# A state-space and feed-forward layer on one core: new order tables for all engines, a third buffer of halves, later weights as five transfers

## The reference, cut to what matters

```python
x = L0_attn_u                                   # (8, 1024, 256), float32
x = x + mixer(layernorm(x))
x = x + ffn(layernorm(x))

def mixer(u):                                   # 8 heads of 64, state 16
    zxbcdt = u @ W_in.T                         # z0, x0, xBC (544), dt (8)
    dt = softplus(dt + dt_bias);  A = -exp(A_log)
    xBC = silu(causal_conv4(xBC) + conv_b)      # x, B, C
    h_t = exp(dt_t A) h_(t-1) + dt_t x_t B_t    # a scan over 1024 positions
    y_t = C_t h_t + D x_t
    y = layernorm(y) * ln_gamma + ln_beta
    y = sigmoid(y @ W_gate.T + b_gate) * y
    return concat(silu(z0) * x0, y) @ W_out.T

def ffn(x):                                     # weights ternary: -1, 0, 1
    h = layernorm(gelu(x @ absmean(W_fc))) * ln_w + ln_b
    return h @ absmean(W_proj)
```

## Time and profile before

| | |
|---|---|
| median of three runs | 1202.77 us (1202.25 to 1202.82) |
| the profiled execution | 1201.22 us; its span 1199.4 us |
| mean granted clock of TensorE | 0.977 |
| PE busy | 1128.5 us (94% of the span), 8534 matmuls |
| DVE busy | 995.9 us (83%) |
| ACT busy | 957.9 us (80%), of it 138.6 us in 108 table loads |
| POOL busy | 406.5 us (34%) |
| chain that ended last | PE 69%, DVE 13%, ACT 6%, DMA 4% |

### The profile page before, as it was taken

The page is one execution under the profiler, slowest core; times in us unless marked ns, Lnnn a source line. Parts: engine busy times, 40 slices in busy tenths (PEclk is TensorE's granted clock), DMA queues, the critical chain, the costliest instruction groups (busy, mean ns, idle before and its releaser), DMA issues.

```text
span 1199.4 us, 23100 instructions
## 1 busy us (share of the span) xinstructions
PE 1128.5 (94%) x8534; PEld 724.5 (60%) x8534; DVE 995.9 (83%) x1958; ACT 957.9 (80%) x1665; POOL 406.5 (34%) x500
## 2 busy tenths in 40 slices
PE   4678999999999999999999999999999999999996
PEld 1345566657576665757666575766657476666663
DVE  5899997989889898988979798988979888676664
ACT  5666587987879888797878988798887878687855
POOL 1111315153343424243341524333243322524341
PEclk9787999999999999999999999999999999999998
DMA  5610202242333424253342434234154320332444
GB/s 150 199 44 11 72 18 64 50 103 45 88 72 58 94 52 98 45 96 67 64 89 51 101 55 94 58 54 107 27 109 78 79 55 8 91 71 65 95 89 106
DMA packets 238976, 89.14 MB, mean 74 GB/s; under 512 B 207760, under 2 KB 235152, under 8 KB 238864
## 3 DMA queue, kind: packets, MB, share of 16 engines
q1 hardware_dynamic: 238864, 87.67, 33.8%
HBM read 24.32 MB, written 8.39 MB: 27 GB/s over the span
## 4 chain that ended last, share of the span: by engine, by line
PE 69%; DVE 13%; ACT 6%; DMA 4%; issue 3%; SPq 3%; POOL 0%; DVEq 0%; ACTq 0%; POOLq 0%
PE bank L360 39%; PE bank L587 8%; PE bank L575 7%; PE bank L509 4%; DVE cv L949 3%; PE bank L518 2%; PE bank L425 2%; PE bank L494 2%; PE bank L526 1%; DMA hT<-hb 1%; DVE EM L1064 1%; SPq L1280 1%; DVE hb L1134 1%; DMA x3T<-hb 1%; PE bank L469 1%
## 5 line engine op out<-in xcount | busy, mean ns | idle before, releaser
L360 PE MATMUL bank<-xnT,win 128*128 128x512 f16 (+1 forms) x1248 | 305.4, 392 | 18.9 <-DMA xnT<-hb 18.2
L360 PEld LDWEIGHTS bank<-xnT,win 128*128 128x128 f16 (+1 forms) x1248 | 124.2, 103 | 153.2 <-issue 34.4
L949 DVE SCALAR_TENSOR_TENSOR cv<-bank,cws,cv 128x510 f32<-128x510 f32 (+5 forms) x240 | 178.8, 745 | 11.2 <-ACT cv L672 2.6
L360 PE MATMUL bank<-yhl,wg 128*128 128x512 f16 x768 | 173.4, 379 | 2.1 <-DVE yhl L1087 2.1
L180 ACT ACT_TABLE_LOAD x108 | 138.6, 1283 | 1.9
L587 PE MATMUL bank<-wpj,hT 128*128 128x256 f16 x1024 | 126.4, 278 | 12.9 <-DMA hT<-hb 12.9
L575 PE MATMUL bank<-wfc,x3T 128*128 128x512 f16 x512 | 127.0, 381 | 4.0 <-DMA x3T<-hb 4.0
L360 PEld LDWEIGHTS bank<-yhl,wg 128*128 128x128 f16 x768 | 73.9, 98 | 92.5 <-issue 4.5
L1206 POOL TENSOR_TENSOR cat<-sz,cat 128x512 f16<-128x512 f32 x64 | 82.6, 1291 | 128.1 <-ACT cat L786 128.1
L1202 POOL TENSOR_TENSOR caty<-tg,caty 128x512 f16<-128x512 f32 x64 | 83.6, 1306 | 118.6 <-ACT caty L774 118.6
L587 PEld LDWEIGHTS bank<-wpj,hT 128*128 128x128 f16 x1024 | 99.7, 99 | 35.3 <-issue 15.6
(11 more groups left out here) (146 smaller groups left out, 2138.2 us busy)
## 6 DMA issues: line engine op xcount, KB each, us to landing
x<-in_x SPq DMA_DIRECT2D x32, 512.0 KB, 4.1
out_y<-x SPq DMA_DIRECT2D x15, 512.0 KB, 3.0
crep<-cv SPq DMA_DIRECT2D x128, 32.0 KB, 2.0
hT<-hb SPq DMA_TRANSPOSE x128, 3.1
caty<-in_wg SPq DMA_DIRECT2D x1, 1024.0 KB, 7.0
x<-in_wout SPq DMA_DIRECT2D x1, 1024.0 KB, 9.4
hT<-in_wfc SPq DMA_DIRECT2D x1, 1024.0 KB, 12.2
hn<-in_wpj SPq DMA_DIRECT2D x1, 1024.0 KB, 13.2
```

Source lines behind the costliest of these rows:

```text
L360: m = eng.matmul(b, lhs(p, k), rhs(q, k), start=(n == 0), stop=(n == len(seq) - 1))
L949: op = eng.scalar_tensor_tensor(cs[0:w, j, 3 - k:T], b[0:w, 0:T - 3 + k], cws[0:w, j, k:k + 1], cs[0:w, j, 3 - k:T], ALU.mult, ALU.add)
```

## The change

All five order tables are new; each holds the same steps with the same parts as before (SP's has five more words, since `W` and `K` now come in parts). Steps of one activation table stand side by side in ScalarE's. `halves` has a third buffer: x keeps `halves[0]`, x2 gets `halves[2]`, and `before_halves0` is gone. `weights` issues one of its five transfers each time that a `W0` comes, `constants` three of its six at each `K0`. Some steps get a further wait. Of the tables the first lines stand here:

```diff
 PE_ORDER = (
-    "c00 z01 u02 c03 c04 v05 c06 c07 z01 v00 m02 c13 x05 z04 x06 x01 u17 e00 s02 c15 b04 q036 x07 c11 g00 c12 "
-    "q053 t06 O07 v04 c11 r002 w0 q067 w0 q053 r046 w0 w0 m17 y05 z03 z10 c22 v04 x16 y07 x11 u20 c26 e14 y05 x12 "
...
+    "c00 c01 u02 v03 c04 z05 c06 c07 z00 m02 z01 c14 v05 c10 x06 x07 x03 v02 u16 x01 e07 s05 c12 c16 c13 q074 g05 "
+    "b07 q004 t01 O05 z00 z17 r042 q016 w0 w0 q035 m11 r063 c25 w0 w0 g11 x14 y02 y00 y07 x16 y03 u24 v02 s16 x11 "
...
 ACT_ORDER = (
-    "a0 h0 W0 N0 W0 c0 z0 c0 b0 c0 a1 h1 c0 10 c0 30 l0 z0 40 s0 s0 50 l0 c1 z0 e0 f0 D0 c1 E0 c1 F0 c1 F0 11 a2 "
-    "h2 E0 31 c1 E0 E0 l0 b1 O0 s1 41 s1 z0 O0 c2 51 y0 z1 c2 y0 e1 f1 E1 y0 c2 y0 E1 n0 c2 l0 n0 12 a3 h3 n0 n0 "
...
+    "N0 a0 h0 W0 W0 c0 c0 c0 a1 10 h1 30 c0 c0 z0 z0 s0 40 b0 s0 l0 c1 50 z0 e0 c1 c1 D0 f0 E0 11 c1 E0 c1 F0 F0 "
+    "a2 O0 h2 31 E0 E0 41 l0 l0 s1 b1 s1 51 z0 z1 c2 y0 y0 f1 y0 E1 E1 e1 y0 12 a3 32 n0 n0 n0 n0 l0 E1 c2 c2 E1 "
...
 DVE_ORDER = (
-    "a0 h0 W0 N0 Z0 W0 a1 c0 u0 c0 v0 00 c0 h1 c0 20 40 c0 v0 50 a2 60 x0 c1 x0 u1 x0 e0 D0 c1 x0 b0 c1 01 g0 c1 "
...
+    "a0 h0 N0 W0 Z0 W0 a1 c0 u0 00 c0 c0 20 h1 40 c0 c0 v0 a2 50 x0 x0 60 v0 v0 u1 x0 c1 01 c1 x0 g0 b0 E0 E0 c1 "
...
 POOL_ORDER = (
-    "a0 a1 l0 H1 a2 l0 c1 c1 c1 c1 l0 c1 y0 y0 y0 y0 a3 l0 k0 k0 k0 k0 y1 H3 a4 c3 y1 c3 y1 y1 c3 c3 l1 c3 k1 l1 "
...
+    "a0 a1 l0 H1 c1 c1 a2 l0 c1 c1 l0 c1 y0 y0 y0 y0 a3 k0 H3 k0 l0 k0 k0 y1 y1 y1 y1 c3 c3 l1 c3 c3 a4 c3 V0 l1 "
...
 SP_ORDER = (
-    "h0 h0 K0 c0 h1 h1 W0 60 h2 h2 c1 61 h3 c2 h3 r0 62 r1 X0 X0 c3 h4 h4 j0 63 j0 j0 j0 j0 j0 j0 j0 c4 X1 X1 p0 "
-    "r2 64 h5 h5 j1 j1 j1 j1 j1 j1 j1 j1 c5 X2 p1 X2 r3 h6 h6 65 j2 j2 j2 j2 j2 j2 j2 j2 X3 X3 c6 p2 h7 h7 r4 j3 "
...
+    "h0 h0 W0 K0 K0 h1 h1 W0 c0 60 W0 W0 h2 h2 c1 61 h3 h3 62 r0 c2 X0 X0 W0 h4 r1 h4 63 c3 j0 j0 j0 j0 j0 j0 j0 "
+    "j0 p0 X1 h5 X1 h5 r2 64 j1 c4 j1 j1 j1 j1 j1 X2 j1 j1 X2 p1 r3 h6 h6 65 j2 c5 j2 j2 j2 j2 j2 j2 X3 X3 c6 j2 "
...
-        halves = [sb(f"hb{n}", [P, 2, 1024], f16) for n in range(2)]
+        halves = [sb(f"hb{n}", [P, 2, 1024], f16) for n in range(3)]
...
-        HALVES0 = [("hx".index(letter), i) for letter, i, _, _ in steps_of(ACT_ORDER) if letter in "hx"]
...
             def bias_rows(i, n, at):
...
+                pe.wait_ge(gam_v, 3)
...
             def half_x(i, n):
...
-                before_halves0(i, 0)
+                act.wait_ge(xt_hi, 16 * i)
+                act.wait_ge(xn_lo, i)
...
             def half_x2(i, n):
...
-                before_halves0(i, 1)
-                eng.activation(halves[0][:, 0, :], x2[:, i % 2].rearrange("p c d -> p (c d)"), ACT.Copy
+                act.wait_ge(x3t_hi, 16 * i)
+                act.wait_ge(x2_lo, i)
+                eng.activation(halves[2][:, 0, :], x2[:, i % 2].rearrange("p c d -> p (c d)"), ACT.Copy
...
-            def before_halves0(i, which):
-                for kind, k in HALVES0[:HALVES0.index((which, i))][-1:]:
-                    act.wait_ge((xt_hi, x3t_hi)[kind], 16 * (k + 1))
-                    act.wait_ge((xn_lo, x2_lo)[kind], k + 1)
...
             def gelu_h(i, n):
...
+                if half == 0:
+                    act.wait_ge(h_sq, at - 1)
...
             def ternary(i, n):
...
+                dve.wait_ge(gam_v, n + 1)
...
             def bias_halves(i, n):
...
+                dve.wait_ge(gam_v, 2)
...
             def var_x(i, n):
...
+                dve.wait_ge(x_var, i)
...
             def rest_x(i, n):
...
-                before_halves0(i, 0)
+                dve.wait_ge(xt_lo, 16 * i)
...
             def rest_x2(i, n):
...
-                before_halves0(i, 1)
-                eng.tensor_tensor(halves[0][:, 1, :], x2[:, i % 2].rearrange("p c d -> p (c d)"), halves[0][:, 0, :],
+                dve.wait_ge(x3t_lo, 16 * i)
+                eng.tensor_tensor(halves[2][:, 1, :], x2[:, i % 2].rearrange("p c d -> p (c d)"), halves[2][:, 0, :],
...
-            def before_halves0(i, which):
-                for kind, k in HALVES0[:HALVES0.index((which, i))][-1:]:
-                    dve.wait_ge((xt_lo, x3t_lo)[kind], 16 * (k + 1))
...
             def dt_last(i, n):
...
+                dve.wait_ge(xd, 4 * (i - 1))
...
             def c_grown(i, n):
...
+                dve.wait_ge(s_done, i)
...
             def b_suffix(i, n):
...
+                dve.wait_ge(seg_l, i + 1)
+                dve.wait_ge(s_done, i)
...
             def gram_mask(i, n):
...
+                dve.wait_ge(em, 4 * i)
...
             def advance(i, n):
...
+                dve.wait_ge(ce, i + 1)
...
             def y_rows(i, j):
...
+                dve.wait_ge(y_lo, 4 * i)
...
             def var_y(i, c):
...
+                dve.wait_ge(y_var, at - 3)
...
+                dve.wait_ge(yn, at - 3)
...
             def var_x2(i, n):
...
+                dve.wait_ge(x2_var, i)
...
             def load_x(i):
...
-            def constants(i, n):
-                for q in range(2):
-                    eng.dma_start(ahl[:, q, :, :, :], c16_d[:, 0:256].rearrange("p (q c r) -> p q c r", q=2, c=NCH)
-                                  ).then_inc(ld_c16, 16)
-                    eng.dma_start(segR[:, q, :, :], c16_d[:, 256:1280].rearrange("p (e t) -> p e t", e=8)
-                                  ).then_inc(ld_c16, 16)
-                    eng.dma_start(pick[:, 2 * q:2 * q + 2, :, :],
-                                  c16_d[:, 1280 + 256 * q:1536 + 256 * q].rearrange("p (c e m) -> p c e m", c=2, e=8)
-                                  ).then_inc(ld_c16, 16)
+            def constants(i, q):
+                eng.dma_start(ahl[:, q, :, :, :], c16_d[:, 0:256].rearrange("p (q c r) -> p q c r", q=2, c=NCH)
+                              ).then_inc(ld_c16, 16)
+                eng.dma_start(segR[:, q, :, :], c16_d[:, 256:1280].rearrange("p (e t) -> p e t", e=8)
+                              ).then_inc(ld_c16, 16)
+                eng.dma_start(pick[:, 2 * q:2 * q + 2, :, :],
+                              c16_d[:, 1280 + 256 * q:1536 + 256 * q].rearrange("p (c e m) -> p c e m", c=2, e=8)
+                              ).then_inc(ld_c16, 16)
...
             def weights(i, n):
...
-                eng.dma_start(wgs, wg_d.rearrange("(k p) n -> p k n", p=P)).then_inc(ld_wg, 16)
-                eng.dma_start(wos, wout_d.rearrange("(k p) n -> p k n", p=P)).then_inc(ld_wout, 16)
-                eng.dma_start(wfs.rearrange("p (k n) -> p k n", k=2), wfc_d.rearrange("(k p) n -> p k n", p=P)
-                              ).then_inc(ld_wfc, 16)
-                eng.dma_start(wps.rearrange("p (k n) -> p k n", k=8), wpj_d.rearrange("(k p) n -> p k n", p=P)
-                              ).then_inc(ld_wpj, 16)
-                eng.dma_start(lnwb[:, :], lnw_d).then_inc(ld_lnw, 16)
+                if n == 0:
+                    eng.dma_start(wgs, wg_d.rearrange("(k p) n -> p k n", p=P)).then_inc(ld_wg, 16)
+                elif n == 1:
+                    eng.dma_start(wos, wout_d.rearrange("(k p) n -> p k n", p=P)).then_inc(ld_wout, 16)
+                elif n == 2:
+                    eng.dma_start(wfs.rearrange("p (k n) -> p k n", k=2), wfc_d.rearrange("(k p) n -> p k n", p=P)
+                                  ).then_inc(ld_wfc, 16)
+                elif n == 3:
+                    eng.dma_start(wps.rearrange("p (k n) -> p k n", k=8), wpj_d.rearrange("(k p) n -> p k n", p=P)
+                                  ).then_inc(ld_wpj, 16)
+                else:
+                    eng.dma_start(lnwb[:, :], lnw_d).then_inc(ld_lnw, 16)
...
             def turn_x(i, n):
...
+                    sp.wait_ge(z_mm, 4 * (i - 2))
...
             def turn_x2(i, n):
...
-                eng.dma_start(x3T[:, n, :, :, :].rearrange("p c k t -> p (c k) t"), halves[0][:, n, :], transpose=True
+                eng.dma_start(x3T[:, n, :, :, :].rearrange("p c k t -> p (c k) t"), halves[2][:, n, :], transpose=True
...
```

## The result

The changed kernel takes 1182.49 us (median of 4 runs, 1182.05 to 1182.58) where the kernel before takes 1202.51 us: 0.9834 of it, 95% interval 0.9818 to 0.9850. A second group of runs gave 0.9832 (0.9815 to 0.9848). The profiled execution took 1182.05 us, its span is 1180.3 us.

A forecast was written before the change was run, and what follows sets the result against it. The prediction took TensorE to bound the middle and VectorE the stretch from 60 to 150 us. From 1201.2 us it took 4 (start), 4 (middle) and 0 (end), giving 1193.2; plus 1.55 for the median, 1195 us (1189 to 1200).

The forecast's parts named there:

- segR, 4.3 us: Start: with later weights in five transfers, TensorE's wait for segR's rows ends at 47.8 instead of 52.1 us, 4.3 us gained.
- the forecast's other reckoning: Start: by ring order wout still delays segR's rows, so splitting the weights gives 2.6 us and not 4.3.
- `ahl`, 2.2 us: Start: the new table order on ScalarE and VectorE removes 2.2 us of TensorE's 4.6 us wait for `ahl`.
- I take 4 us as gained at the start: Start: of 4.3 + 2.2 us, 4 us come through because VectorE is nearly full from 60 to 150 us; ends 0 and 11.
- VectorE's table now puts 3 us less work ahead of `y2`.: Start: moving `D0` and other steps leaves VectorE 176.4 instead of 179.4 us of work before its `y2` step.
- The half clock: Up to 180 us: some 36 us run at 1.2 GHz; if early holes close, TensorE holds 2.4 GHz for longer.
- Table loads, 0 us: ScalarE: switches fall from 108 to 95, 16.7 us less, hidden behind TensorE's fixed 948 us and so costed at 0.
- rival D: Whole kernel: the compiler keeps more than 95 table loads; within 2 us of the forecast, no chance of its own.
- rival A: Whole kernel: all 16.7 us of ScalarE's loads return, 1186 us; chance 0.20, shared with a start gaining over 8 us.
- The middle, -6.6 + 2.6: 180 to 1140 us: waits for hT, x3T and yhl go (6.6 us), late banks cost 2.6; -4, ends -15 and +12.
- rival C: Middle: bursts on TensorE's banks make 61 more hand-backs late, 0.3 us each, 18 us; slower at 1214.5 us, chance 0.24.
- The end, 0 us, at most 2 lost: Last block: two more gelu ahead of the first `j` (0.5 us later), one store fewer between transposes (0.3 us); 0, -1 to +2.

The follow-up runs named there:

- the kernel above with its mark at 187.2 us: Changed kernel with every second table load issued twice, which left the same 95 loads in the profile: 1182.61 us, 0.9834 of the kernel before.
- the delayed hT: 40 small transfers ahead of h's first transposes, blocks 3 to 12: changed kernel 1181.24 us (0.9818 of the kernel before), kernel before 1203.82 us (1.0007).
- two buffers in turn: Changed kernel with the last block's halves of h for chunks 1 and 3 in halves[0] instead of halves[1]: 1178.57 us, 0.9806 of the kernel before.

## Why the forecast was right in its direction and wrong in its size

*segR, 4.3 us.* The walk was right nearly to the tenth: segR's rows are issued at 42.47 us (42.6 forecast), and the first `q0` starts at 47.4 us (47.8). Undoing the split costs 6.2 us at the mark. wout, still ahead of the rows in the queue, was issued at 33.52 us and took 6.7 us to land, so it was out of their way; the 1.7 us that the forecast's other reckoning charged for it did not show.

*`ahl`, 2.2 us.* Forecast: `10` at about 29.0 us; measured 29.02, where it stood at 32.69. TensorE's wait fell by 3.1 us. Undoing it (3.07 us later) costs 4.3 us at the mark. (The forecast's list of new steps ahead of the first `q0` lacks one more `v0`; its count of 25 and its 5.4 us are right.)

*"These 4.3 + 2.2 us don't come through in full", and then "I take 4 us as gained at the start". This step failed.* The start gave 12.5 us by TensorE and 14.6 us by VectorE's mark. 6.5 us had been found; undone one at a time, the two edits cost 6.2 and 4.3 us at the mark, and 4.5 to 5 us each by the medians, so they came through whole and more. The forecast read VectorE's 85.4 busy of 90 us as a reason for taking an early start back. It is the reverse: an engine that is full hands a shift of its first instruction on to its last one. What could take a shift back is idle time behind it, and in the new orders that did not grow (9.4 us, 9.2 with either edit undone). In the old orders the split by itself was worth only 1.3 us, so there the forecast's doubt held; whether idle time took the rest is not shown (13.9 to 16.1 us without the split, 16.6 with it). The forecast took its idle time from 60 to 150 us alone; 18.6 us of it lay before 60 us, where the two edits act.

*"VectorE's table now puts 3 us less work ahead of `y2`."* The forecast mentioned it and then added nothing for it. It measured 5.5 us, and a us of VectorE's work near 80 us is worth half a us to a us at the end (4.9 us for 5.2 us in the kernel before; 2.4 us by the medians, 3.9 us at the mark, for 4.5 us in the changed one). The new orders, beside that, took 4.5 us of VectorE's idle time behind 60 us. The 4 us are close to the third share, 4.6 us of idle time before 60 us; the other two had no term. The start's term should have been 12.5 to 14.6 us, outside its own ends of 0 and 11. Its sign, the u step of block 3 about 4 us earlier, came out at 13 us (144.2 to 130.9). The case had a chance in the forecast, within the 0.20 for "A, or a start that gains more than 8 us".

*The half clock.* The forecast had it as a hope. Up to 180 us the time at 1.2 GHz fell by 11 us (0.90 to 0.93). It lies within the 14.6 us, not on top of them, and the kernel above with its mark at 187.2 us in spite of a lower clock speaks against a large part; no run tests it by itself.

*Table loads, 0 us.* Right within about 1 us, and all 13 are gone (so not rival D). The Trainium skill (ScalarE: Activation LUTs, Table sets: the hidden batching unit) says to batch calls by set and not by function; rival A took all of the 16.7 us to come back by it. The time that A named, 1186 us, is nearer to the result than the forecast, but its mechanism is refuted where it was counted: 13 loads put back cost about 1 us. Where a load stands ahead of a chain that the start waits for, as ahead of `10`, two of them with a silu cost 4.5 us: what counts is the place of a switch, not their number.

*The middle, -6.6 + 2.6.* In idle time this was right: it fell by 4.1 us (11.35 to 7.3). The waits for hT and x3T went, that for yhl grew from 1.1 to 2.0 us. The banks took what they were charged: TensorE's waits for a bank rose from 0.6 us (two, for `v30` and `v50`) to 3.0 us (1.65 for `p40`, 1.0 for `zc1`, two of under 0.2). Behind the wait of `p40` the granted clock was 0.50 from 515.2 to 518.5 us, and the step took 3.2 us from start to start where others take 1.75. So rival C's mechanism is there, far below its 18 us. (The forecast's own factors, 60 hand-backs, one in five late by 0.2 us, give 2.4 us and not 2.6.) What had no term is the rest of the 8.4 us: pauses of TensorE that lie under the modelled ends, also in front of `r`, `q` and `n`, and one stretch at half clock instead of two (at 852 and 937 us in the kernel before). That the grown distances did this was not shown: the delayed hT fits it by its waits, but not by the time.

*Third buffer 0, added waits 0.* Right: 0.9994 for the buffer alone.

*The end, 0 us, at most 2 lost.* It lost 1.8 us, inside its ends. From the first matmul of the last `f` steps to the end of the span it is 30.2 us after and 29.9 before, so the chain that I had looked at was right. What is lost lies ahead of it: TensorE waits 0.47 and 2.66 us for hT of block 14, and the `p` behind it runs at 1.2 GHz, 3.48 instead of 1.91 us. In the kernel before, it waited 1.22 us for hT and 1.32 us for x3T, at full clock:

```profile
1166.32 1.91 PE L587 MATMUL bank<-wpj,hT 128*128 128x256 f16 x16 [1.22 <-DMA hT<-hb]
1169.55 5.34 PE L575 MATMUL bank<-wfc,x3T 128*128 128x512 f16 x24 [1.32 <-DMA x3T<-hb]
```

These are 2.2 us.

In sum, by TensorE: start -12.5 (forecast -4), middle -8.4 (-4), end +1.8 (0): -19.1 us of span. The direction was no luck, since both terms had it; of the 11 us of span that the forecast lacks, 8.5 lie in the start and 4.4 in the middle, less the 1.8 at the end.

## What to carry to other kernels

In this case an engine that was full didn't absorb an early start, it handed it on; count the idle time in front of the full stretch and the work that leaves it as gains, and subtract only idle time that could grow behind. Do it for the new order as a whole: the same edit was worth 1.3 us in the old one and 5 us in the new one. Price a table load by what waits behind it on its own engine: ahead of a chain at the start its full length counted, amid a full TensorE one eighth. At the end of a program look for a buffer that is used in turn with itself: other buffers are free by then, and here that gave 3.5 us in a version that is faster than both kernels (1178.6 us). And count an added instruction in the profile before believing that it costs nothing.

## What the runs showed of the hardware

A single VectorE instruction can take over 1 us where its like takes 0.68. This is the group of yhl in the changed kernel (min, median and max in ns):

```profile
L1092 DVE TENSOR_TENSOR yhl<-yT,yhl x64: 676/682/1640, 100.0 to 1110.1; 128x512 f16<-128x512 f32 x64
```

In the changed kernel 55 instructions of VectorE lie 0.25 us or more above the median of their form, 43 us in all. Each of the 55 overlaps an instruction of GpSimd, though only 685 of VectorE's 1958 do, and 52 of them have two inputs in SBUF. The other 630 that overlap one are not held up so. ScalarE has none, before or after. The Trainium skill (Advanced Engine Details and Errata, GPSIMD Details) says that GpSimd shares a read and a write interface with VectorE and conflicts with VectorE instructions that have two SBUF inputs; the trace agrees, without showing which of the overlapping ones are hit. The two kernels hardly differ in it (59 such instructions and 46 us before), so it explains at most little of the change.

TensorE's granted clock falls at the end after waits: in the changed kernel sixteen matmuls of `p` took 3.48 to 3.53 us behind three waits of 2.3 to 3.0 us, 2.44 us behind one of 2.73 us, and 1.91 us behind one of 0.92 us. It isn't the length of the last wait alone: with two buffers in turn they took 1.91 us behind 2.73 and 2.03 us.
